# Two-stage cross-attention on one core: phi G of two batches as one product, and v from spread context sums

## What is computed

```python
q, k, v = h @ w_q.T, ctx @ w_k.T, ctx @ w_v.T
probs = softmax(q @ k.T / sqrt(512))
x1 = h + alpha * (probs @ v) @ w_o.T
g_x     = (g_w @ ctx + g_b).T                 # 512 x 128
theta_x = (theta_w @ x1 + theta_b).T          # 512 x 128
phi_x   = phi_w @ ctx + phi_b                 # 128 x 512
y   = ((theta_x @ phi_x / 512) @ g_x).T
out = batch_norm(w_w @ y + w_b) + x1
```

## Time and profile before

| what | value |
|---|---|
| median of 3 runs | 389.10 us (389.08 to 389.27) |
| the profiled execution | 389.22 us, its span 387.3 us |
| PE busy | 382.2 us (99%) |
| DVE busy | 306.8 us (79%) |
| ACT busy | 199.1 us (51%) |
| POOL busy | 1.3 us |
| granted clock of PE | 0.999 |
| matmuls | 1827 |

### The profile page before, as it was taken

The page is one execution under the profiler, slowest core; times in us unless marked ns, Lnnn a source line. Parts: engine busy times, 40 slices in busy tenths (PEclk is TensorE's granted clock), DMA queues, the critical chain, the costliest instruction groups (busy, mean ns, idle before and its releaser), DMA issues.

```text
span 387.3 us, 5597 instructions
## 1 busy us (share of the span) xinstructions
PE 382.2 (99%) x1827; PEld 321.5 (83%) x1827; DVE 306.8 (79%) x596; ACT 199.1 (51%) x411; POOL 1.3 (0%) x6
## 2 busy tenths in 40 slices
PE   8999999999999999999999999999999999999995
PEld 5888888888888888888888888888888888888885
DVE  4899788986698677986798867985798867986786
ACT  3477567432764257542665247451675338451553
POOL 1000000000000000000000000000000000000000
PEclk9999999999999999999999999999999999999999
DMA  8975742485474646546383555655375464024523
GB/s 244 376 294 211 268 122 54 157 297 189 131 247 119 234 136 216 187 139 217 107 269 111 190 169 167 231 158 187 120 241 161 162 190 135 27 82 154 145 83 108
DMA packets 56507, 68.13 MB, mean 176 GB/s; under 512 B 4656, under 2 KB 47408, under 8 KB 53424
## 3 DMA queue, kind: packets, MB, share of 16 engines
q1 hardware_dynamic: 55776, 67.07, 52.6%
q10 hardware_dynamic: 720, 0.92, 0.7%
HBM read 49.09 MB, written 18.87 MB: 175 GB/s over the span
## 4 chain that ended last, share of the span: by engine, by line
PE 96%; DMA 1%; DVE 1%; ACT 0%; ACTq 0%; issue 0%
PE bank L354 23%; PE bank L355 23%; PE bank L356 23%; PE bank L408 8%; PE bank L427 7%; PE bank L394 5%; PE bank L416 4%; PE bank L449 2%; DMA cT_raw<-w_q 1%; PE bank L453 1%; DVE xb L1095 0%; DVE xb L1090 0%; ACTq L614 0%; ACT t_sides L611 0%; ACT theta_hi L611 0%
## 5 line engine op out<-in xcount | busy, mean ns | idle before, releaser
L355 PE MATMUL bank<-c_sides,qk_hi 128*128 128x512 f32 x128 | 49.9, 390 | 0.0
L356 PE MATMUL bank<-c_sides,qk_lo 128*128 128x512 f32 x128 | 49.9, 390 | 0.0
L354 PE MATMUL bank<-ov_hi,c_sides 128*128 128x512 f32 x128 | 49.9, 390 | 0.0
L355 PE MATMUL bank<-ov_lo,c_sides 128*128 128x512 f32 x128 | 49.9, 390 | 0.0
L354 PE MATMUL bank<-c_sides,qk_hi 128*128 128x512 f32 x128 | 49.8, 389 | 0.0
L356 PE MATMUL bank<-ov_hi,c_sides 128*128 128x512 f32 x128 | 49.8, 389 | 0.0
L611 ACT ACTIVATE t_sides<-bank 128x512 fp32r<-128x512 f32 x32 | 19.0, 594 | 37.6 <-PE bank L356 37.6
L408 PE MATMUL bank<-t_sides,xT_hi 128*128 128x512 f32 x128 | 31.9, 391 | 0.0
L611 ACT ACTIVATE probs<-bank 128x512 f32<-128x512 f32 x16 | 9.4, 586 | 38.6 <-PE bank L416 38.6
L845 DVE TENSOR_TENSOR t_sides<-bank,t_sides 128x512 fp32r<-128x512 f32 x32 | 22.0, 687 | 8.9 <-ACT t_sides L611 8.9
L704 ACT ACTIVATE probs<-probs,neg_max 128x256 f32<-128x256 f32 x32 | 16.1, 502 | 24.1 <-DVE neg_max L961 24.1
(11 more groups left out here) (147 smaller groups left out, 835.9 us busy)
## 6 DMA issues: line engine op xcount, KB each, us to landing
cT_raw<-ctx_t SPq DMA_DIRECT2D x8, 1024.0 KB, 5.9
xT_raw<-x_t SPq DMA_DIRECT2D x8, 1024.0 KB, 4.8
c_raw<-ctx_n SPq DMA_DIRECT2D x8, 1024.0 KB, 6.8
xb<-x SPq DMA_DIRECT2D x16, 512.0 KB, 4.1
out<-xb SPq DMA_DIRECT2D x14, 512.0 KB, 2.8
gram_moved<-gram_blocks SPq DMA_DIRECT2D x16, 256.0 KB, 2.3
gram_blocks<-gram_moved SPq DMA_DIRECT2D x64, 64.0 KB, 2.0
moved<-blocks SPq DMA_DIRECT2D x16, 256.0 KB, 2.3
```

Of the source, the lines that this page charges most:

```text
L354: pe.matmul(dst, ahi, bhi, start=(k == 0), stop=False)
L355: pe.matmul(dst, ahi, blo, start=False, stop=False)
L356: mm = pe.matmul(dst, alo, bhi, start=False, stop=(k == k_tiles - 1))
```

## The change

1. `gram_raw` and `gram` lose the two extra columns. `gram` is laid out with the two batches side by side for each row block, and `phi_gram` makes one product of 512 columns for both, into one bank: 6 matmuls a pair for 12. It waits for the low parts of both batches' G.
2. The context's sums are in a tile of their own, `c_sum`. SP stores them in DRAM (`send_sums`) and reads them back spread over all 128 partitions as rows of 512 (`fetch_sums`), into the room of the batch-norm rows, which are no longer needed then.
3. DVE multiplies these rows with phi's rows (`weigh_sums`, `phi_rows`, a new load of 128 KB at the start); ACT adds each row up with `accum_out` (`v_sums`), which gives v. phi_bias is divided by 256, since it is now added to each of the 256 terms.
4. `phi_squares` is one transpose of 512 columns.
5. In SP's order `load_c` of pair 0 goes ahead of G's squares.

```diff
-        gram_raw = sb("gram_raw", [P, 2, KS, GW])
-        gram = split("gram", [P, 2, KS, GW])
+        gram_raw = sb("gram_raw", [P, 2, KS, S])
+        gram = split("gram", [P, KS, 2, S])
+        c_sum = sb("c_sum", [P, 2 * KS])
+        phi_rows = sb("phi_rows", [P, S])
+        sums_moved = nc.dram_tensor("sums_moved", [2, P, KS], F32).ap()
+        sum_rows = row[:, ROW_GAMMA:ROW_GAMMA + 2 * S].rearrange("p (b s) -> p b s", b=2)
...
+            def send_sums():
+                sp.dma_start(sums_moved.rearrange("b p k -> p b k"), c_sum[:].rearrange("p (b k) -> p b k", b=2)).then_inc(sums_stored, 16)
+            def fetch_sums():
+                sp.dma_start(row[:, ROW_GAMMA:ROW_GAMMA + 2 * S],
+                             sums_moved.rearrange("b p k -> (b p k)").partition_broadcast(P)).then_inc(sums_loaded, 16)
...
+            sp.dma_start(phi_rows[:], phi_n).then_inc(phi_rows_loaded, 16)
...
             load_c(1)
+            send_sums()
+            sp.wait_ge(sums_stored, 16)
+            sp.wait_ge(bn_step, 8)
+            fetch_sums()
...
+                def next_sums():
+                    sp.wait_ge(sums_stored, turned[32])
+                    sp.wait_ge(v_made, two[2])
+                    fetch_sums()
...
+                if not last:
+                    sp.wait_ge(c_summed, four[8])
+                    send_sums()
                 if prefetch:
-                    if not first:
-                        sp.wait_ge(c_summed, four[8])
-                        load_c(p + 2)
+                    load_c(p + 2)
+                if not last:
+                    next_sums()
+                if prefetch:
                     sp.wait_ge(cT_lo, two[4])
                     load_cT(p + 2)
...
-            def phi_gram(b, banks=PHI_BANK):
-                product(bank[banks[b]][:, 0:GW], lambda k: cut(phi_w, every, k, every),
-                        lambda k: cut(gram, every, b, k, every), KS).then_inc(phi_done, 1)
+            def phi_gram(to_bank):
+                product(bank[to_bank][:].rearrange("p (b s) -> p b s", b=2), lambda k: cut(phi_w, every, k, every),
+                        lambda k: cut(gram, every, k), KS).then_inc(phi_done, 1)
...
-                    pe.wait_ge(v_made, two[2])
+                    pe.wait_ge(phi_turned, p + 1)
                 for st in range(KS):
                     values(0, st)
...
-                for b in range(2):
-                    pe.wait_ge(gram_lo, two[b + 3])
-                    phi_gram(b)
+                pe.wait_ge(gram_lo, two[4])
+                phi_gram(PHI_BANK)
...
+                def v_sums():
+                    act.wait_ge(sums_weighted, two[2])
+                    for b in range(2):
+                        act.activation(sum_rows[:, b], sum_rows[:, b], ACT.Identity, bias=phi_bias[:],
+                                       accum_out=v[:, b:b + 1]).then_inc(v_made, 1)
...
+                if not first:
+                    v_sums()
                 low_scores(0)
...
                 cT_parts(loads[32])
                 if first:
+                    v_sums()
                     u_part()
                     c_sums(loads[32])
...
-                def phi_squares(b, count, banks=PHI_BANK):
+                def phi_squares(count, from_bank):
                     dve.wait_ge(phi_done, count)
-                    dve.transpose(phi_blocks[:, :, b * KS:(b + 1) * KS].rearrange("p j x a -> p x j a"),
-                                  bank[banks[b]][:, 0:S].rearrange("p (k j i) -> p k j i", k=KS, i=SQUARE)
-                                  ).then_inc(phi_blocks_made, 1)
-                    dve.tensor_scalar(v[:, b:b + 1], bank[banks[b]][:, S:S + 1], phi_bias[:], None,
-                                      ALU.add).then_inc(v_made, 1)
+                    dve.transpose(phi_blocks[:].rearrange("p j x a -> p x j a"),
+                                  bank[from_bank][:].rearrange("p (x j i) -> p x j i", x=2 * KS, i=SQUARE)
+                                  ).then_inc(phi_turned, 1)
+                def weigh_sums():
+                    dve.wait_ge(sums_loaded, loads[16])
+                    if first:
+                        dve.wait_ge(phi_rows_loaded, 16)
+                    for b in range(2):
+                        dve.tensor_tensor(sum_rows[:, b], sum_rows[:, b], phi_rows[:], ALU.mult).then_inc(sums_weighted, 1)
...
+                if not first:
+                    weigh_sums()
                 row_maxima(0)
...
                 vo_part(1, 1)
                 if first:
+                    weigh_sums()
                     u_rows()
```

More of the change, by code:

```diff
@@ L289, in pair @@
                     send_squares(0)
-                    sp.wait_ge(phi_blocks_made, two[2])
+                    sp.wait_ge(phi_turned, 1)
                     send(phi_moved, phi_blocks[:], phi_stored)
@@ L317, in pair @@
                 if prefetch:
-                    if first:
-                        sp.wait_ge(c_summed, four[8])
-                        load_c(p + 2)
                     sp.wait_ge(xT_lo, two[4])
@@ L332, in pair @@
                     store(p, 0)
-                    sp.wait_ge(phi_blocks_made, two[4])
+                    sp.wait_ge(phi_turned, turns[2])
                     send(phi_moved, phi_blocks[:], phi_stored)
@@ L691, in pair @@
                 loads = counts(act, p, 16, [32])
-                landed = counts(act, p, 16 * BLOCKS, [16 * BLOCKS])
+                landed, pairs_done = counts(act, p, 16 * BLOCKS, [16 * BLOCKS]), counts(act, p, 1, [1])
                 two, four = counts(act, p, 2, [-1, 0, 1, 2, 3]), counts(act, p, 4, range(-2, 9))
@@ L827, in pair @@
                 theta_part(1)
-                act.wait_ge(c_summed, four[8])
                 for b in range(2):
-                    gram_part(b, four[4 + KS * (b + 1)], two[b + 1])
+                    gram_part(b, four[4 + KS * (b + 1)], pairs_done[1])
                 tT_part(2, four[7])
@@ L998, in u_rows @@
                             at = phi_blocks[:, :, b * KS + k]
-                            dve.scalar_tensor_tensor(out=at, in0=phi_b, scalar=gram_raw[:, b, k, S:S + 1], in1=at,
+                            dve.scalar_tensor_tensor(out=at, in0=phi_b, scalar=c_sum[:, b * KS + k:b * KS + k + 1], in1=at,
                                                      op0=ALU.mult, op1=ALU.add).then_inc(u_made, 1)
@@ L1168, in pair @@
                 tT_part(3, four[8])
-                phi_squares(0, two[3])
-                phi_squares(1, two[4])
+                phi_squares(pairs_done[2], PHI_BANK)
                 out_rows(1, 0)
@@ L1182, in _ @@
             pool.memset(g_bias[:], 1.0).then_inc(ones_made, 1)
-            pool.memset(gram_raw[:], 0.0).then_inc(pad_zeroed, 1)
 def kernel(**inputs):
@@ L1209 @@
         "g_w": a[l1 + "g_w"],
+        "phi_n": a[l1 + "phi_w"].reshape(CI, KS, P).transpose(0, 2, 1).reshape(CI, S),
         "phi_w_t": a[l1 + "phi_w"].T,
```

38 lines of the change are left out of this document (19 added, 19 removed).

## The result

The changed kernel takes **394.06 us** (median of 6 executions, 392.11 to 395.16); the kernel before took 389.15 beside it (388.98 to 389.46). The ratio is 1.0122, 95% interval 1.0108 to 1.0136: **slower by 4.9 us**. The profiled execution took 394.26 us, its span is 392.5 us, 5.2 more than before. The prediction of 389.0 us was wrong, and the time lies above its range of 388.3 to 389.9.

The account below looks back on a forecast made before the run. PE's stream of products was taken to bound the kernel. The profiled 389.22 - 0.56 (phi G) + 0.41 (pair 0) gave 389.07, less 0.12 for the median 388.95, so 389.0 us; range 388.3 to 389.9.

Parts of the forecast that it names:

- PE's own part: phi G on PE: six products of 512 columns for 12 of 258 save 0.07 us, 8 times, -0.56 us.
- The new work at the start of a pair: Pairs 1 to 7: DVE's multiplications (0.67 us) and ACT's sums (1.0 us) fit in idle time, cost 0.
- Pair 0, DVE's shift: Pair 0: multiplications delay DVE by 0.67 us; PE waits 0.26 for u's low part, 0.15 for x1, +0.41 us.
- SP and the DMAs: SP's queue: the sums' store, wait and fetch delay G's squares up to 1 us, within slack, cost 0.
- The start: Kernel start: phi's rows ahead of the context's first load, 0.4 us of transfer, covered by ACT's idling, cost 0.
- Rival D: Pair 0: store slowed by the following 1 MB load, G's squares late, PE stalls 2.3 us: 391.3 us, chance 0.11.
- B: Rival for pair 0: DVE's shift is hidden too, no short waits of PE: 388.5 us, chance 0.14.
- C: Rival for phi G: only the columns are gained, 0.08 us saved and about 0.45 lost: 389.5 us, chance 0.11.
- A: The forecast itself for the whole kernel: 389.0 us, no change, chance 0.60.

Follow-up runs that it names:

- SP's part alone: Kernel before plus only SP's new store, wait and spread fetch, with zeros stored as the sums and the arithmetic unchanged: 395.72 us, ratio 1.0158.
- the run without the store: Kernel before with SP's new orders but no store of the sums and no wait for it, one context row fetched spread: 389.61 us, ratio 1.0010.
- the rows apart: Kernel before with SP's new store, wait and fetch, the fetch reading 128 different context rows instead of one row 128 times: 393.44 us, ratio 1.0102.
- c's load last: Changed kernel with only c's 1 MB load of pair 0 moved back behind G's squares: 394.75 us, ratio 1.0123.

## Why the prediction was wrong, by its steps

- **PE's own part** (-0.56). Right in kind. From pair 2 on, a pair takes 44.29 us for 44.34 or 44.35: 0.055, not 0.07, and phi G of pair 1 ran from 135.05 to 136.44, 1.39 us for six products, not 1.36. Over 8 times that is 0.44. By N / 2.4 + 2.5 ns, which the Trainium skill (TensorE: Matmul & The Clock Gate, "Back-to-back issue gap") gives for the gap of a matmul by itself, an estimate is 0.025 a pair; the trace stands nearer to the rows of before.
- **The new work at the start of a pair** (0). Right. In pair 2 the multiplications start at 138.68 and take 0.75 by their row, the sums on ACT 1.1 us from 139.47, and both are done ahead of the scores: ACT's copy of them still waits 0.75 us for PE, DVE 2.51 for ACT.
- **Pair 0, DVE's shift** (+0.41). The 0.67 is exact; the waits are 0.4 and 0.3 where 0.26 and 0.15 were said. The rest goes with the 0.5 us by which the squares of pair 0 came late, which the next step had missed: SP's part alone, without the multiplications, has waits of 0.5 us for x1 and 0.3 for v o's low part.
- **SP and the DMAs** (0): **the step that failed**, in the sentence "A store to DRAM of 256 KB lands after 2.3 us. I take this for the small one", and in what it says of G's squares a few sentences on: "they may land up to 1 us late". The small store lands after 3.6 us in pair 0; 5.8 us is the median of the eight. So the columns' load was issued at 71.39, not 69.8. The squares were issued at 74.43, not 73.67, and took 6.8 us, not 3.3 at most: they landed 5.3 us late, more than the slack, and the cost was not 0 but 2.8 us of standstill and 1.7 of clock. Ahead of pair 0 too: "stored near 49" was 50.1, and the squares that "as before" should go at 50.21 went at 50.46. The row of 256 KB was no guide to this store. Nor was the page: the Trainium skill (DMA: Bandwidth & Descriptors, "Anatomy of one DMA") gives its about 2 us of fixed time for transfers issued from GpSimd, and this one is SP's. Where the store stood in pair 0 with no load just ahead of it, it took 3.3 to 4.0 us with 8-byte pieces, and 1.4 with 16-byte pieces.
- **The start** (0). Right. The first scores of pair 0 start at 41.99 us; before, at 42.14.
- **Rival D** had the path, the place and the sign, with a chance of 0.11, and gave 391.3. Its condition did not come true: the store took 3.6 us and not over 4.5, and landed at 71.0, not 74.1; SP waited 2.7 us for it in pair 0, not over 4. That its standstill of 2.3 us is near the 2.8 measured is partly luck: it had G's squares take 5.3 us behind the columns, and they took 6.8, which made up for the earlier store. The size of the whole is off by its other half: D priced a stall of 2.3 us, and the stall was 2.8; it left out that PE's clock fell behind the standstill, 1.7 us, and the 0.3 of the late squares of pair 0, the 0.3 in pair 1 and the 0.1 by which the saving is smaller. 391.3 + 0.5 + 1.7 + 0.3 + 0.3 + 0.1 = 394.2, about what was measured. Its reason for the slow store was wrong: not the 1 MB behind the store holds it (with none there it takes 3.3 us in pair 0), but how its 2 KB are cut into pieces, as the runs with 16-byte pieces show.
- B and C did not come into play. The range was made from A, B and C "with D outside": a step that leans on "no row shows" a store of such pieces, with a row of 128 times the size as its only guide, deserved the bound of its rival inside the range.

## What to carry to other kernels

Price a small transfer by its pieces too, not by its bytes alone: 2 KB in 8-byte pieces took 3.6 us where 256 KB in rows took 2.3, and a wait for them in a queue delays every load behind it, which then collides with the next thing on the critical path. Let each partition write what it has as one piece, store early, and put the wait where the data is used. And set a gain of 0.05 us a pair against what its detour can cost once: here a standstill of PE of 2.8 us, and 1.7 us more for the clock that fell after it.

## What the runs showed of the hardware

- The window of the transfers right after the small store in pair 0, 67 to 71 us, in 40 slices of 0.1 us (GB/s moved in each, and all packets of the window):

```profile
GB/s 0 0 0 0 0 0 0 0 0 0 0 0 0 10 10 1 0 0 0 573 82 0 0 0 492 164 0 0 0 0 0 0 0 0 0 0 0 0 0 246
DMA packets 291, 0.16 MB, mean 39 GB/s; under 512 B 272, under 2 KB 272, under 8 KB 272
```

The small packets go at 68.3 to 68.6; the 1 MB load, issued at 67.83, has little to show by 71: all that moved in the window is 0.16 MB. The store landed at 71.0. Without a store ahead of it, 0.66 MB had moved in the 3.2 us behind the issue of the same load, in the run without the store. So the store holds up what stands behind it in the queue. That it does so until it lands is not shown: with 16-byte pieces in the changed kernel the store had landed at 68.08, and the load, issued at 67.05, had still moved only 0.19 MB by 70.25.
- The store's time varied with what was in flight, from 3.6 to 8.0 us in one execution. With 16-byte pieces and the same order the median was 4.6 to 4.7 us, and in pair 0 it was 1.4. In the later pairs of the changed kernel the stores took 4.6 to 6.7 us, and no pair from 2 on was longer for it.
- Whether the clock falls behind a standstill can't be told from its length in these runs. Before phi G of pair 0, PE waited 2.3 us with SP's part alone, and the granted clock was 0.55 to 0.60 for the 4 us from 89 on; with the rows apart it waited 2.1 us and the clock stayed at 1.00; with c's load last it waited 2.0 and the clock fell to 0.51. The windows of PE from 89 to 91 us, with SP's part alone and then with the rows apart:

```profile
89.00:91.00 2.00, 2.00 (x12) 0.55 0.32 135
```

```profile
89.00:91.00 2.00, 2.00 (x12) 1.00 0.00 0
```

So waits of about the same length end at either level. The six executions of the changed kernel fit the price of 1.7 us: with a granted clock of 1.0 their spans are 390.3, 391.7 and 392.0 us, with 0.993 to 0.996 they are 392.5, 393.0 and 393.4.
